# One tile place of eight in an input ring is loaded by two DMAs, of 120 and of 8 partitions

## The chip, the core and the metric

The kernel runs on one core of one Trainium2 chip. The metric is the device time of one execution in microseconds. Five engines with their own instruction streams work side by side: PE (TensorE, with its weight load PEld), DVE (VectorE), ACT (ScalarE), POOL (GpSimd) and SP (SyncE), which here only issues DMAs and waits. The core has 16 DMA engines that all queues share.

## The reference, cut to what matters

```python
def ref(inputs):                                   # inputs: (2048, 64, 256) float32
    Z = jnp.einsum('bnd,bmd->bnm', inputs, inputs) # a 64x64 Gram matrix per batch
    li, lj = jnp.tril_indices(n, k=-1)             # n = 64: strictly below the diagonal
    return Z[:, li, lj]                            # (2048, 2016)
```

## The kernel before, in words

The input is 134.2 MB (128 tiles of 1 MB), the output 16.5 MB. A tile is 16 batches: 128 partitions, each with 8 joined rows of 256 floats, which is one run of 8 KB in DRAM. `x_joined` is the input seen in this way, so that tile t is rows `t * PARTS` to `(t + 1) * PARTS`.

**Loads.** SP issues one DMA a tile (L151) into place `k = t % 8` of the ring `x_in`. The ring has eight places, each with a semaphore `loaded[k]` that the DMA raises by 16. From tile 8 on, SP waits before each load until DVE has turned the tile that used the place before (L147). Tiles 4 and 5 wait for the multiplications of tiles 0 and 1 (`LATE`, L150).

**DVE.** `turn(t)` waits for `loaded[k]` (L195), then for PE to be done with the tile that used this place of `x_turned` three tiles earlier (L197), and transposes the tile in 32x32 blocks from `x_in` to `x_turned` (L198). From tile 11 on, `turn_rows` follows every second tile: it transposes one of four pieces of a group's products (L215). A group is eight tiles.

**PE.** A hardware loop of 43 laps with three tiles each; the places of tiles run over 129, of which the first is blank. A tile is 256 matmuls (L252), placed side by side in the array. PE waits for `turned[j]`, and before the end of a set for the other PSUM set to be emptied.

**ACT** copies the products out of PSUM (`keep`, L279), packs part of the rows into `packed_rows` (`pack`, L120 and L126) and issues two store DMAs a group (L137). **POOL** carries the parts that change partitions (L131). The last group's stores are issued by SP in four DMAs.

The order of work on each engine is written out in the program. What changes lies in SP's `load` and in the wait of DVE's `turn`.

Of the kernel before, what the change touches and what calls it, by code (L numbers as in the profile page):

```python
# [7 lines left out]
PARTS = 128  # L8
# [6 lines left out]
def first_column(i):  # L15

    return i * (i - 1) // 2


def gram_lower_triangle(nc: bass.Bass, x: bass.AP, y: bass.AP):  # L20
# [10 lines left out]
    TILE = SIDES * PER_SIDE  # L31
    TILES = BATCHES // TILE
    IN_RING = 8


    LATE = {4: 0, 5: 1}
# [29 lines left out]
    x_joined = x.rearrange("b (i r) d -> (b i) (r d)", r=JOINED)  # L66

    with ExitStack() as stack:  # L68
        def sbuf(name, shape):
            return stack.enter_context(nc.sbuf_tensor(name, shape, F32))  # L70

        def semaphore(name):
            return stack.enter_context(nc.semaphore(name))

        x_in = sbuf("x_in", [PARTS, IN_RING, JOINED * DIM])

# [9 lines left out]

        loaded = [semaphore(f"loaded{k}") for k in range(IN_RING)]

# [13 lines left out]
        def place(t):  # L102

            return divmod(t + BLANK, LAP)

        def set_of(j):

            return (0, j) if j < SET_TILES[0] else (1, j - SET_TILES[0])

        def piece_rows(piece):  # L110
            return slice(ROWS - (piece + 1) * PIECE, ROWS - piece * PIECE)

        def wait_packed_free(engine, group):

            if group >= 2:
                engine.wait_ge(stored[group % 2], group // 2 * STORES)
# [11 lines left out]
        def carry_across(copy, group, i, side):  # L128

            first, at = side * HALF, first_column(i)  # L130
            return copy(packed_rows[first:first + BLOCK, group % 2, :, at + BLOCK:at + i],  # L131
                        row_halves[first + BLOCK:first + HALF, i, :, 0:i - BLOCK])

        def store(engine, group, columns):
            rows = y[group * GROUP:(group + 1) * GROUP, columns].rearrange("(h q s) c -> s q h c", h=RUNS, s=SIDES)
            for side in range(SIDES):
                engine.dma_start(rows[side],  # L137
                                 packed_rows[side * HALF:side * HALF + BLOCK, group % 2, :, columns]).then_inc(
                    stored[group % 2], 16)

        @block.sync
        def _(sync):
            def load(t):
                k = t % IN_RING
                if t >= IN_RING:
                    lap, j = place(t - IN_RING)
                    sync.wait_ge(turned[j], (lap + 1) * LAP)  # L147
                elif t in LATE:
                    lap, j = place(LATE[t])
                    sync.wait_ge(tile_multiplied[j], (lap + 1) * ARRAY_TILES)  # L150
                sync.dma_start(x_in[:, k], x_joined[t * PARTS:(t + 1) * PARTS]).then_inc(loaded[k], 16)  # L151

            for t in range(TILES):
                load(t)

            group, long_rows = GROUPS - 1, first_column(BLOCK)
            sync.wait_ge(packed_home, group * PIECES + LONG_PIECES)
            sync.wait_ge(packed_across, (group + 1) * LONG_PIECES)
            sync.wait_ge(last_carried, 1)
            store(sync, group, slice(long_rows, PACKED))  # L160
            sync.wait_ge(packed_home, GROUPS * PIECES - 1)
            sync.wait_ge(last_packed, 1)
            store(sync, group, slice(0, long_rows))
            for b in range(2):
                groups = (GROUPS - b + 1) // 2
                sync.wait_ge(stored[b], (groups + (1 if group % 2 == b else 0)) * STORES)
# [23 lines left out]
        @block.vector  # L190
        def _(dve):
            def turn(t):

                k, (lap, j) = t % IN_RING, place(t)
                dve.wait_ge(loaded[k], (t // IN_RING + 1) * 16)  # L195
                if lap > 0:
                    dve.wait_ge(tile_multiplied[j], lap * ARRAY_TILES)  # L197
                nc.vector.transpose(  # L198
                    x_turned[:, j].rearrange("p c b s (h u n v) -> p u v (c b s h) n", h=ROWS // BLOCK, u=PAIRS, v=PAIR),
                    x_in[:, k]).then_inc(turned[j], LAP)  # L200

            def turn_rows(n):
                group, piece = divmod(n, PIECES)
                rows = piece_rows(piece)
                if piece == 0:

                    lap, j = place((group + 1) * GROUP_TILES - 1)
                    s = set_of(j)[0]
                    dve.wait_ge(kept[s], (lap + 1 + s) * LAP)
                if group > 0:  # L210

                    dve.wait_ge(packed_home, n - PIECES + 1)
                    if piece < LONG_PIECES:
                        dve.wait_ge(packed_across, (group - 1) * LONG_PIECES + piece + 1)  # L214
                nc.vector.transpose(  # L215
                    row_halves[:, rows].rearrange("p i h (n u v) -> p (i h) u n v", u=PAIRS, v=PAIR),
                    products[:, group % KEPT_RING, rows, :].rearrange("p i (h q) -> p (i h) q", q=BLOCK)).then_inc(
                    rows_turned, 1)

            for j in range(BLANK):  # L220
                nc.vector.memset(x_turned[:, j, 0:CHUNKS // 2], 0.0).then_inc(turned[j], 1)  # L221
            turned_rows = 0
            for t in range(TILES):
                turn(t)
                if t >= PIECE_LAG and (t - PIECE_LAG) % 2 == 0:
                    turn_rows(turned_rows)
                    turned_rows += 1
            for n in range(turned_rows, GROUPS * PIECES):
                turn_rows(n)
            wait_packed_free(dve, GROUPS - 1)  # L230
            dve.wait_ge(rows_turned, (GROUPS - 1) * PIECES + LONG_PIECES)
            for i in range(BLOCK + 1, ROWS):
                last = carry_across(nc.vector.tensor_copy, GROUPS - 1, i, 1)
            last.then_inc(last_carried, 1)
# [105 lines left out]
```

## Time and profile before

| What | Value |
|---|---|
| Median of 3 runs | 417.86 us (416.99 to 419.29) |
| Profiled execution, its own time | 417.85 us |
| Its span, first to last instruction | 416.1 us |
| Mean granted TensorE clock | 0.959 |
| Busy: PE, PEld, DVE | 377.6, 370.4, 364.5 us |
| Busy: ACT, POOL | 178.8, 199.9 us |
| Moved by DMA | 151.01 MB, mean 363 GB/s |

The span is what the trace covers; 1.75 us of the execution's own time lie around it. Times in rows are microseconds from the span's start. Releasers (after `<-`) are what ended an engine's idle time. Busy shares are averages over a start, a long middle and an end that have different limits, so the stretches have to be read one by one.

### The profile page before, as it was taken

To read this page: it belongs to the slowest core of one execution; us is meant where nothing else is said; L and a number is where in the kernel's file an instruction comes from. 1 tells how busy PE (TensorE), PEld (TensorE's weight loads), DVE (VectorE), ACT (ScalarE), POOL (GpSimd) and SP (SyncE) were. 2 spreads that over 40 slices of the span, in tenths; PEclk is the share of its full clock that TensorE was granted. 3 is DMA by queue.
4 is the path that set the end of the run, shared out by engine and by line. 5 is a ranking of instruction groups with operands and counts; after the bars stand their busy time and mean duration, and the time that the engine had idled before them with its cause. 6 is when DMAs were issued, how large, how long until landed. Compare 5 with 4: busy or idle time off the path is not lost.

```text
span 416.1 us, 68691 instructions
## 1 busy us (share of the span) xinstructions
PE 377.6 (91%) x33024; PEld 370.4 (89%) x33024; DVE 364.5 (88%) x224; ACT 178.8 (43%) x829; POOL 199.9 (48%) x981
## 2 busy tenths in 40 slices
PE   4469999999999999999999999999999899899940
PEld 4469999999999999999999999999999899898940
DVE  3438899999999999999999998999979799797964
ACT  0011134434555434554345543455544445444465
POOL 1000084664818283564828183563808356182783
PEclk9559999999999999999999999999999999999985
DMA  8259999999999999999999999999999999995218
GB/s 325 87 181 425 426 419 425 418 423 421 420 421 423 423 421 421 422 420 423 380 423 399 388 419 411 403 380 415 347 425 338 422 382 358 392 326 247 68 50 199
DMA packets 21178, 151.01 MB, mean 363 GB/s; under 512 B 2592, under 2 KB 2720, under 8 KB 4768
## 3 DMA queue, kind: packets, MB, share of 16 engines
q1 hardware_dynamic: 18752, 135.26, 81.3%
q10 hardware_dynamic: 2400, 15.48, 9.9%
q14 instruction: 20, 0.16, 0.1%
q8 instruction: 6, 0.10, 0.1%
HBM read 134.22 MB, written 16.52 MB: 362 GB/s over the span
## 4 chain that ended last, share of the span: by engine, by line
PE 55%; DMA 31%; DVE 5%; issue 5%; ACT 2%; ACTq 0%; DVEq 0%
PE bank_set L252 55%; DMA x_in<-x_dram 31%; DVE x_turned L198 4%; ACT packed_rows L120 1%; DVE row_halves L215 1%; ACT packed_rows L126 1%; DVE x_turned L221 0%; ACTq L137 0%; ACT products L279 0%; DVEq L197 0%; ACTq L68 0%; DVEq L214 0%; ACTq L294 0%; ACTq L270 0%
## 5 line engine op out<-in xcount | busy, mean ns | idle before, releaser
L252 PE MATMUL bank_set<-x_turned 32*64 32x64 f32 x33024 | 377.6, 236 | 22.7 <-issue 11.9
L252 PEld LDWEIGHTS bank_set<-x_turned 32*64 32x64 f32 x33024 | 370.4, 132 | 29.8 <-issue 22.6
L198 DVE STREAM_TRANSPOSE x_turned<-x_in 128x2048 f32<-128x2048 f32 x128 | 292.0, 2290 | 41.2 <-PE bank_set L252 18.0
L131 POOL COPY packed_rows<-row_halves 32x60 f32<-32x60 f32 (+30 forms) x961 | 196.4, 206 | 209.2 <-DVE row_halves L215 171.6
L279 ACT COPY products<-bank_set 128x512 f32<-128x512 f32 (+1 forms) x91 | 68.6, 760 | 208.6 <-PE bank_set L252 189.3
L215 DVE STREAM_TRANSPOSE row_halves<-products 128x1024 f32<-128x1024 f32 x64 | 77.1, 1207 | 3.2 <-ACT products L279 2.7
L120 ACT COPY packed_rows<-row_halves 128x32 f32<-128x32 f32 (+30 forms) x481 | 62.8, 220 | 0.0
L126 ACT COPY packed_rows<-row_halves 128x128 f32<-128x128 f32 x256 | 56.9, 300 | 4.3 <-issue 3.0
L279 ACT ACT_TABLE_LOAD x1 | 1.3, 1283 | 19.9 <-PE bank_set L252 19.9
L131 DVE COPY packed_rows<-row_halves 32x2 f32<-32x2 f32 (+30 forms) x31 | 3.4, 187 | 0.0
L120 POOL COPY packed_rows<-row_halves 128x2 f32<-128x2 f32 (+14 forms) x15 | 2.3, 210 | 0.1
L221 DVE MEMSET x_turned<- 128x1024 f32 x1 | 0.9, 912 | 1.0 <-PEq L334 1.0
L172 POOL MEMSET x_turned<- 128x1024 f32 x1 | 1.0, 952 | 0.4 <-POOLq L334 0.4
L334 POOL MEMSET const-float32-0.0<- 128x1 f32 x1 | 0.1, 99 | 0.2 <-issue 0.2
L334 POOL MEMSET const-bfloat16-1.0<- 128x1 bf16 x1 | 0.1, 102 | 0.0
L334 POOL MEMSET const-uint8-127<- 128x1 uint8 x1 | 0.1, 102 | 0.0
L334 POOL MEMSET const-float32-1.0<- 128x1 f32 x1 | 0.1, 99 | 0.0
## 6 DMA issues: line engine op xcount, KB each, us to landing
x_in<-x_dram SPq DMA_DIRECT2D x128, 1024.0 KB, 17.3
y_dram<-packed_rows ACTq DMA_DIRECT2D x30, 504.0 KB, 8.1
y_dram<-packed_rows SPq DMA_DIRECT2D x2, 380.0 KB, 3.9
y_dram<-packed_rows SPq DMA_DIRECT2D x2, 124.0 KB, 3.6
```

Of the source, the lines that this page charges most:

```text
L120: return copy(packed_rows[:, group % 2, :, at:at + i], row_halves[:, i, :, 0:i])
L126: return copy(two[:, :, :, 0:BLOCK], row_halves[:, i:i + 2].rearrange("p w h j -> p h w j"))
L131: return copy(packed_rows[first:first + BLOCK, group % 2, :, at + BLOCK:at + i], row_halves[first + BLOCK:first + HALF, i, :, 0:i - BLOCK])
L172: nc.gpsimd.memset(x_turned[:, j, CHUNKS // 2:CHUNKS], 0.0).then_inc(turned[j], LAP - 1)
L198: nc.vector.transpose(x_turned[:, j].rearrange("p c b s (h u n v) -> p u v (c b s h) n", h=ROWS // BLOCK, u=PAIRS, v=PAIR), x_in[:, k]).th ...
L215: nc.vector.transpose(row_halves[:, rows].rearrange("p i h (n u v) -> p (i h) u n v", u=PAIRS, v=PAIR), products[:, group % KEPT_RING, row ...
L221: nc.vector.memset(x_turned[:, j, 0:CHUNKS // 2], 0.0).then_inc(turned[j], 1)
L252: done = nc.tensor.matmul(bank_sets[s][side * HALF:(side + 1) * HALF, g, at, :].rearrange("r (n u v) -> r u n v", u=PAIRS, v=PAIR), rows, ...
L279: last = nc.scalar.copy(products[:, group % KEPT_RING, :, in_group * PER_SIDE:(in_group + count) * PER_SIDE].rearrange("p i (m g b) -> p i ...
L334: nc = bacc.Bacc("TRN2", target_bir_lowering=False, num_devices=1)
```

## The change

The tile in place 4 of the ring (tiles 4, 12, ..., 124: 16 of the 128) is loaded by two DMAs from SP, one right after the other: partitions 0 to 119, then 120 to 127. Both raise the same semaphore by 16, and DVE's wait counts 32 a lap for this place. Everything else stays.

```diff
+    SPLIT, AHEAD = 4, 120
...
-                sync.dma_start(x_in[:, k], x_joined[t * PARTS:(t + 1) * PARTS]).then_inc(loaded[k], 16)
+                first = t * PARTS
+                if k == SPLIT:
+                    sync.dma_start(x_in[0:AHEAD, k], x_joined[first:first + AHEAD]).then_inc(loaded[k], 16)
+                    sync.dma_start(x_in[AHEAD:PARTS, k], x_joined[first + AHEAD:first + PARTS]).then_inc(loaded[k], 16)
+                else:
+                    sync.dma_start(x_in[:, k], x_joined[first:first + PARTS]).then_inc(loaded[k], 16)
...
-                dve.wait_ge(loaded[k], (t // IN_RING + 1) * 16)
+                dve.wait_ge(loaded[k], (t // IN_RING + 1) * (32 if k == SPLIT else 16))
```

## Rows read from the trace of the kernel before

**Rows 1.** The page, part 2: the span in 40 slices, busy tenths and GB/s

```profile
PE   4469999999999999999999999999999899899940
DVE  3438899999999999999999998999979799797964
DMA  8259999999999999999999999999999999995218
GB/s 325 87 181 425 426 419 425 418 423 421 420 421 423 423 421 421 422 420 423 380 423 399 388 419 411 403 380 415 347 425 338 422 382 358 392 326 247 68 50 199
```

**Rows 2.** The chain that ended last, in order of time: start, length, what

```profile
36.81 8.63 PE bank_set L252 x422
45.44 0.12 issue
...
229.56 5.99 PE bank_set L252 x294
...
241.32 20.79 DMA x_in<-x_dram
...
366.00 21.77 DMA x_in<-x_dram
...
391.67 8.83 PE bank_set L252 x423
```

**Rows 3.** The tile x_in, its instructions and landings, stretch 280:400

```profile
L198 DVE STREAM_TRANSPOSE x_turned<-x_in x38: 2268/2272/2315, 280.0 to 394.0; 128x2048 f32<-128x2048 f32 x38
  DMA x_in<-x_dram: 6.9, 7
DMA to landing us min/median/max: 19.7/21.6/24.7
```

**Rows 4.** The tile x_in, its landings, stretch 75:100

```profile
DMA to landing us min/median/max: 12.5/13.5/15.5
```

**Rows 5.** Windows: columns named in the first line; share of the 16 DMA engines

```profile
core 0: us, PE busy (x) PEld busy (x) DVE busy (x) ACT busy (x) POOL busy (x), PEclk, DMA share, GB/s
180.00:200.00 20.00, 19.76 (x1775) 19.50 (x1773) 19.38 (x11) 8.36 (x41) 10.21 (x49) 1.00 1.01 422
24.30:26.50 2.20, 0.47 (x29) 0.28 (x19) 0.00 (x0) 0.00 (x0) 0.00 (x0) 0.50 0.05 22
383.00:384.00 1.00, 1.00 (x121) 1.00 (x107) 1.00 (x1) 0.00 (x0) 0.00 (x0) 1.00 0.06 25
391.00:392.00 1.00, 0.88 (x85) 0.75 (x72) 1.00 (x2) 0.39 (x3) 0.84 (x5) 1.00 0.06 25
```

**Rows 6.** DMA packets in the stretch 383:391

```profile
DMA packets 29, 0.21 MB, mean 27 GB/s; under 512 B 3, under 2 KB 3, under 8 KB 3
```

**Rows 7.** The page, parts 2 and 3: packets and queues of the whole span

```profile
DMA packets 21178, 151.01 MB, mean 363 GB/s; under 512 B 2592, under 2 KB 2720, under 8 KB 4768
q1 hardware_dynamic: 18752, 135.26, 81.3%
q10 hardware_dynamic: 2400, 15.48, 9.9%
q14 instruction: 20, 0.16, 0.1%
```

**Rows 8.** SP's own waits and its issue of loads over the span

```profile
SPq L151 <- DVE x_turned L198: 301.1, 116, 4.7
L151 SPq DMA_DIRECT2D x_in<-x_dram x128: 327/328/662, 0.7 to 371.5; - x128
```

**Rows 9.** All engines in order of time, stretch 0:45; idle before in brackets

```profile
26.53 18.72 PE L252 MATMUL bank_set<-x_turned 32*64 32x64 f32 x1551 [1.75 <-issue]
...
27.65 2.31 DVE L198 STREAM_TRANSPOSE x_turned<-x_in 128x2048 f32<-128x2048 f32 x1 [5.42 <-PE bank_set L252]
```

**Rows 10.** DVE in order of time, stretch 396:416.1

```profile
401.20 3.75 DVE L215 STREAM_TRANSPOSE row_halves<-products 128x1024 f32<-128x1024 f32 x3 [2.69 <-ACT products L279]
```

## The prediction

> **What bounds the kernel now.** I read the slices of the page first [rows 1]. After a start of some 30 us, PE and the DMA engines are both at 9 tenths, and DVE nearly so, up to about 380 us. But in the last third PE and DVE have slices at 8 and 7 tenths, while GB/s falls from a flat 420 to values between 338 and 425. Three resources that are all "busy" need the chain to tell them apart.
>
> The chain [rows 2] has two parts. From 36.81 to 229.56 us it is PE alone: 22 laps of three tiles, (229.56 - 36.81) / 22 = 8.761 us a lap, 2.920 us a tile, with 0.12 us of loop issue in each. PE is the bound there, at a granted clock of 1.00 [rows 5]. From 241 us on the chain is loads: pieces of 21 to 22 us from the issue of a load to its landing. Lap 42, the last, starts at 391.67. From 229.56 that is 162.11 us for 18 laps (two laps lie before 36.81, then 22, 18 and the last make 43), or 9.006 us a lap instead of 8.761. So the second part lost 162.11 - 18 x 8.761 = 4.41 us to late loads. That the loads are late and not DVE is seen in the turns: 38 turns start between 280.0 and 394.0 us, 114.0 / 37 = 3.08 us apart, while DVE idled 6.9 us for loads [rows 3].
>
> **Why loads are late although the DMA engines still move data quickly.** A load took 13.5 us from issue to landing between 75 and 100 us [rows 4] and 21.6 us after 280 [rows 3]. SP issues as soon as a place is free, so this is the age of a load in a ring of eight tiles. Such a growth can't come from a mean rate: at 422 GB/s [rows 5] a tile of 1.049 MB takes 2.485 us, under PE's 2.920. With a group's stores (2 x 64 x 8,064 B = 1.032 MB, 2.45 us) eight tiles need 8 x 2.485 + 2.45 = 22.3 us against PE's 23.4. The mean has 1 us to spare in a group; one member has not. The end of the load stream shows it. The last load is issued at 371.5 [rows 8]. From 383 to 392 the share of the 16 DMA engines is 0.06, at 25 GB/s [rows 5]: 1/16 = 0.0625, one DMA engine alone. In 383:391 it moves 26 packets of 8 KB and 3 completion packets [rows 6], 8 / 26 = 0.308 us each: full speed for one, since 422 / 16 = 26.4 GB/s is 0.310 us for 8 KB. So the other 15 are done with all tiles while one still has about 10 us of work, some four tiles. The same signature stands at 24.30:26.50, share 0.05 [rows 5], in the early tile that is issued alone. I call it the late engine. A tile counts as landed only with its share, so the late engine sets DVE's time.
>
> Its pace: 8 x 3.08 = 24.6 us for eight tiles, of which 64 load packets take 64 x 0.308 = 19.7; the other 4.9 are 8 store packets and what it loses besides. That is 1.3 us over PE's 23.4. It falls behind in every group, the ring hides it until about 235 us, and then it leads.
>
> **What the change does.** Packets are one partition row each: 128 loads x (128 rows + 16 completions) and 4 stores x (64 + 16) give 18752, the count of q1 [rows 7]. So a whole tile is 8 rows on each of 16 engines. The trace has no load of 120 rows. Bounds for what the late engine carries of a split tile: nothing (120 = 15 x 8, the grain of the whole tile kept, and one engine left out), or 9 rows (the same, and one of the 8 single rows on top). In the first case it saves 8 x 0.308 = 2.46 us in eight tiles, in the second it gets 0.31 more. I keep both ends and choose the first; the second and the middle are rivals.
>
> The Trainium skill, "DMA: Bandwidth & Descriptors", section "Why a DMA increments its semaphore by 16 and not by 1", says that a DMA is spread over the largest number up to 16 that divides the slowest dimension, on the lowest-numbered engines. By it, 120 rows go to engines 0 to 14 and the 8 rows to engines 0 to 7, one each; engine 15 gets none. No row here carries an engine's number. The same page, in "Latency and other measured facts", calls engines 7 and 15 usually slower: if the late one is 15 the sum is the first end, if it is 7 the second.
>
> *The late engine, first end:* 24.6 - 2.46 = 22.1 us for eight tiles, under PE's 23.4 by 1.3 us; the loss per group is gone, and the lag never fills the ring.
>
> *The engines with 9 rows:* mean pace 22.3 + 0.31 = 22.7 us. The page puts q10 at 9.9% of 416.1 us, 41.2 us for 30 stores [rows 7], 1.37 us each instead of 1.22, so 2.75 in a group: 8 x 2.485 + 0.31 + 2.75 = 22.9 us. It is under 23.4, by 0.4 us.
>
> *SP:* one more issue of 0.33 us in eight tiles, 16 in all [rows 8]. SP is waiting 301.1 us for DVE [rows 8]; behind the second issue stands the next load, whose place comes free 2.9 us later, and loads are issued 12 us and more before DVE wants them. Cost nothing; if that cover were gone, 0.33 us for each of 16 tiles, 5 us. The further completion packets are a few ns each.
>
> *DVE:* the wait only counts to 32, no instruction more. It waits for the later of two landings. The 8 rows are queued right behind the 120, so they are a packet's time late, 0.3 us, hidden by the ring's age of 13 us. The Trainium skill, same page, "Rules for kernel authors", speaks against such a pair: it wants 128 partitions and 1 MiB in a DMA and says that two transfers to disjoint partitions bring nothing. By it only the 0.3 us a split tile and no gain would be left, the rival "no change".
>
> *Start:* tiles 0 to 3 are not split. DVE turns tile 4 at 27.65, released by PE and not by the load, and PE works without a break from 26.53 on [rows 9], so an earlier landing of tile 4 is worth nothing. *End:* after PE's last lap (391.67 + 8.83 = 400.50) come ACT's copy, four turns of rows on DVE from 401.20 [rows 10], packing and stores, 416.1 - 400.5 = 15.6 us, none of it a load. It moves as a block.
>
> *DVE as next bound:* for eight tiles 8 x 2.272 [rows 3] and four turns of rows of 1.25 (3.75 us for three, [rows 10]) are 23.2 us, close to 23.4. But in 180:200, where no load is late, DVE does just this with 19.38 of 20 us busy [rows 5] and PE keeps its pace. So PE leads to the end.
>
> **Sum.** PE's last lap starts at 229.56 + 18 x 8.761 = 387.26 instead of 391.67. The span becomes 416.1 - 4.4 = 411.7, and the execution's own time 417.85 - 4.4 = 413.4 us. The profiled execution's time is the median's (417.86), so no further shift.
>
> **The rivals.**
> - *The late engine is among those with 9 rows (slower).* It is at work without a break from about tile 5 until 392.5, so each packet more moves the end of its work: 15 x 0.31 = 4.7 us. PE's last laps hang on it, 422.5 us. For: nothing in the rows says which engine is late, and eight of 16 would carry more. It decides as soon as the late engine's share of a split tile is above 8. Against: it would have to be one of those eight.
> - *Its share stays at 8, or the split is spread otherwise and relieves nobody in particular:* 417.9 us. For: seven of the 16 are in this place in the likeliest split.
> - *The late engine is relieved, but those with 9 rows take over.* Needs 0.5 us in a group beyond my 22.9: for example the 20 instruction packets [rows 7] falling on them, or the unexplained loss at stores. Each 0.15 us over 23.4 costs about 2 us over 15 groups: 415.5 us.
> - *Too little relief:* it needs 1.3 of the 2.46 us, five rows of eight, to be under PE. With four rows taken off, 24.6 - 1.23 = 23.4, the gain is still nearly whole.
>
> **How the numbers follow.** Late engine left out and PE leads: 0.70, 413.4, own range 412.3 to 414.8. Relieved but with a new leader: 0.05, 415.5. No change: 0.11, 417.9. Slower: 0.14, 422.5. The 0.70 is a judgement: no row gives an engine's number, and a blind draw would make it 1 in 16. I put it far higher because both facts single out one engine: one alone of 16 is late all through the run, and the likeliest split leaves out one alone, at an end of the row. A measurement of this kernel can tell about 0.5%, 2.1 us. Faster 0.74 (the first two), same 0.12, slower 0.14. The range runs from 412.3 to 418.5 and leaves out the slower case and little else. The low end adds 1 us for the tail, where POOL's carries could start earlier.
>
> **What would show it.** Completion packets: 2592 under 512 B now, 162 DMAs x 16; with 15 + 8 instead of 16 in each of 16 tiles it should be 2592 + 16 x 7 = 2704; with 16 in each, 2848. The chain should be laps of 8.76 us up to the last, starting near 387.3. The turns after 280 should be 2.92 us apart, waits for loads near nothing, and the age of loads after 280 no longer above that of 75:100. The stretch with share 0.06 before the last landing should be gone. If share 0.06 lasts longer than 10 us, the slower rival is right; if 24.6 us for eight tiles stays, the second. A short share of 8/16 at the end would be the engines with the ninth row.

## The result and the profile after

The changed kernel takes 490.6 us (median of 6 runs, 486.0 to 493.0), the kernel before 417.5 us beside it: ratio 1.174, 95% interval 1.170 to 1.178. It is 73 us slower; forecast were 413.4 us and a range up to 418.5. The profiled execution took 486.0 us, its span is 484.2. Where a result below says "one run", a second run was left out because the chip was in a slower state.

The page of the kernel after, part 2, same columns as [rows 1], with the granted clock:

```profile
PE   4579998989979797888887797879978787897960
DVE  4348697969687787968587794878779687886974
PEclk8569999997999899889989898998989999898995
DMA  8369999999999999999999999999999999999136
GB/s 338 86 224 420 296 403 291 420 316 413 285 403 319 382 294 384 321 343 363 299 372 250 377 290 319 378 247 400 267 388 327 315 366 256 391 276 349 53 87 171
```

The row to read is GB/s. The DMA engines are as busy as before, 9 tenths throughout, but from the fifth slice to the sixteenth the rate alternates between about 290 and 400, one slice each. A slice is 12.1 us, two are 24 us, about eight tiles: once in a lap of the ring the same engines take longer for the same bytes. A busy share doesn't show this; busy share and GB/s side by side do.

The chain of the kernel after, in order of time (start, length, what):

```profile
57.37 2.32 DVE x_turned L206
60.10 21.05 DMA x_in<-x_dram
81.15 1.42 issue
82.56 2.32 DVE x_turned L206
...
397.05 1.14 issue
398.19 2.32 DVE x_turned L206
...
459.70 8.84 PE bank_set L260 x426
```

Loads lead from 32.8 us on (75% of the span), not from 241 [rows 2]. The step from one turn of a split tile to the next is (398.19 - 57.37) / 12 = 28.4 us for eight tiles, against PE's 23.4 and the late engine's 24.6. PE's last lap starts at 459.70 instead of 391.67 [rows 2]: 68.0 us later, the whole difference of the spans (484.2 - 416.1 = 68.1). The tail moved as a block, as forecast.

Windows around the second split tile, tile 12, in the kernel after (columns as in [rows 5]):

```profile
45.00:48.00 3.00, 2.83 (x266) 2.70 (x257) 2.70 (x2) 1.13 (x2) 0.00 (x0) 1.00 1.01 415
48.00:51.00 3.00, 3.00 (x292) 3.00 (x280) 1.74 (x1) 0.00 (x0) 0.00 (x0) 1.00 1.07 208
51.00:54.00 3.00, 3.00 (x292) 3.00 (x285) 1.71 (x1) 0.66 (x1) 0.00 (x0) 1.00 1.04 197
54.00:57.00 3.00, 2.86 (x272) 2.73 (x261) 1.73 (x2) 0.94 (x2) 1.02 (x5) 1.00 0.94 339
```

For six microseconds all 16 engines are busy at half the rate, 208 and 197 GB/s. The packets and the waits of the kernel after:

```profile
DMA packets 21290, 151.01 MB, mean 312 GB/s; under 512 B 2704, under 2 KB 2832, under 8 KB 4880
q1 hardware_dynamic: 18864, 135.26, 82.8%
PEld bank_set L260 <- DVE x_turned L206: 65.6, 52, 2.6
DVE x_turned L206 <- issue: 59.0, 38, 3.5
```

The bytes are the same and the completion packets are 2704, the number forecast for 15 + 8 engines in each split tile. So the spread over the engines was as the first end of my bounds assumed; what it costs was not. DVE's 59.0 us "issue" are waits for loads that the profile gives no releaser for: each of the 38 ends 0.08 us after a landing in the place that DVE turns next. Only 14 of them, 17.2 us, stand before split tiles; 24, 41.8 us, stand before whole ones. The whole tiles are late as well. PE now waits for DVE, and after it starved a lower clock is granted, as in this stretch of the kernel after:

```profile
438.00:440.00 2.00, 0.11 (x8) 0.11 (x16) 2.00 (x2) 1.31 (x5) 1.68 (x9) 0.90 1.01 396
440.00:442.00 2.00, 2.00 (x142) 2.00 (x145) 2.00 (x2) 0.00 (x0) 1.01 (x6) 0.50 1.00 407
```

PE works 0.11 of 2 us, and the next 2 us are granted at 0.50, the lower of the clock's two levels (1.2 of 2.4 GHz). Its busy time grew from 377.6 to 392.6 us.

### The profile page after: what moved, and what is told of

Same layout as the page of the kernel before. It is cut to its first block, busy times and chain, and to the rows that moved or that the text cites. A ratio compares the mean times of both kernels' runs of the same rounds, so it can differ in the third digit from the quotient of the medians.

```text
span 484.2 us, 68707 instructions
## 1 busy us (share of the span) xinstructions
PE 392.6 (81%) x33024; PEld 381.2 (79%) x33024; DVE 366.0 (76%) x224; ACT 179.3 (37%) x829; POOL 198.2 (41%) x981
## 2 busy tenths in 40 slices
DMA packets 21290, 151.01 MB, mean 312 GB/s; under 512 B 2704, under 2 KB 2832, under 8 KB 4880
## 4 chain that ended last, share of the span: by engine, by line
DMA 75%; DVE 8%; issue 7%; PE 6%; ACT 2%; SPq 1%; ACTq 0%; DVEq 0%
DMA x_in<-x_dram 75%; DVE x_turned L206 7%; PE bank_set L260 6%; ACT packed_rows L123 1%; SPq L156 1%; ACT packed_rows L129 1%; DVE row_halves L223 1%; SPq L159 0%; DVE x_turned L229 0%; ACTq L140 0%; ACT products L287 0%; ACTq L71 0%; DVEq L205 0%; ACTq L302 0%; ACTq L278 0%
## 5 line engine op out<-in xcount | busy, mean ns | idle before, releaser
L260 PE MATMUL bank_set<-x_turned 32*64 32x64 f32 x33024 | 392.6, 242 | 75.8 <-DVE x_turned L206 58.3
L260 PEld LDWEIGHTS bank_set<-x_turned 32*64 32x64 f32 x33024 | 381.2, 137 | 87.0 <-DVE x_turned L206 65.6
```

The costliest lines, as they stand in the source:

```text
L260: done = nc.tensor.matmul(bank_sets[s][side * HALF:(side + 1) * HALF, g, at, :].rearrange("r (n u v) -> r u n v", u=PAIRS, v=PAIR), rows, ...
```

## The experiments

All kernels are the kernel before with one edit in SP's `load` (and the count in DVE's wait). Ratios are to the kernel before on the same chip; the chips differ between groups of runs. `PIECES_OF` lists the pieces that place 4 is loaded in, `aside` is a tensor that nobody reads. The diffs are cut to the line that matters. The expectations speak of ports: SBUF, the on-chip memory that holds `x_in`, is reached through ports that each serve certain partitions, and the theory is that DMA engines which write one port at the same moment share its rate. The mapping follows in the point on the step that failed.

**1. Which of the two DMAs costs: 120 alone, 128 + 8, 112 + 16, 64 + 64.**

```diff
                 if k == SPLIT:
+                    for a, b in PIECES_OF:    # e1: (0,120); e2: (0,128); e3: (0,112),(112,128); e4: (0,64),(64,128)
+                        sync.dma_start(x_in[a:b, k], x_joined[first + a:first + b]).then_inc(loaded[k], 16)
+                    # e2 only: 8 rows more
+                    sync.dma_start(aside[120:128], x_joined[first:first + 8]).then_inc(loaded[k], 16)
...
```

> Place 4 is loaded by the 120-partition DMA alone; partitions 120 to 127 of that place are loaded once, with tile 4, and left out afterwards (15 of 16 tiles). Theory A: the DMA of 120 partitions is itself slow, because its packets take about twice their time (in the changed kernel's trace half the stretches run at 200 GB/s, the others at 420). Then most of the loss stays: 465 to 490 us. Theory B: the DMA of 8 partitions is what hurts. Then this one goes back to 413 to 419 us. Theory C: two DMAs on one semaphore, or the wait for 32, cost the time: back to 413 to 419 us as well.

e1: 479.1 us (one run; the kernel before 417.2). 120 alone keeps some 62 of the 73 us.

> Place 4 is loaded whole by one DMA of 128, and a second DMA brings 8 rows more to a tensor that nobody reads; DVE waits for both. Theory A (the 120 is slow): 417 to 424 us, the 8 rows cost a packet or so on the engines that carry them. Theory B (the 8 are slow): 450 us and more. Theory C (two DMAs on one semaphore): 450 us and more.

e2: 426.3 us, ratio 1.021 (1.015 to 1.028). 2 us above theory A's range. The 8 rows cost 9.1 us, not 4.7, but a small part of the loss; two DMAs on one semaphore are no cause of the rest. 62 + 9 = 71, nearly the 73.

> Place 4 is loaded by DMAs of 112 and of 16 partitions; both divide by 16, so completion packets should be 32 a split tile (2848 under 512 B in all). Theory A1: a DMA is slow when its rows don't spread over all 16 engines (120 on 15). Then 112 and 16 are both fine: 415 to 421 us. Theory A2: a DMA is slow when its share of rows for each engine is a contiguous block that doesn't match how the partitions are joined to the memory's ports; only the whole tile of 128 is laid out to match. The Trainium skill, 'SBUF — State Buffer', section 'Door 1', gives the mapping; by it 112 in blocks of 7 collides often. Then this kernel is slow as well: 440 to 490 us.

e3: 471.7 us (one run), completion packets 2848: 16 engines for both DMAs, and slow all the same. Theory A1 (too few engines) falls.

> Place 4 is loaded by two DMAs of 64 partitions, 0 to 63 and 64 to 127, each on 16 engines with 4 rows. Theory A1 (fewer than 16 engines is what is slow): 415 to 421 us, no loss. Theory A2 (ports): by the skill's mapping partitions 0 to 63 reach only half of the ports, and so do 64 to 127, so each DMA runs at half speed: the tile takes about 5 us instead of 2.5 and the kernel 450 to 480 us. Completion packets 2848 in both.

e4: 484.5 us, ratio 1.161 (1.147 to 1.174), completion packets 2848. The windows from 48 to 54 us in this run:

```profile
48.00:51.00 3.00, 3.00 (x288) 3.00 (x283) 2.28 (x1) 0.20 (x1) 0.00 (x0) 1.00 1.09 243
51.00:54.00 3.00, 3.00 (x292) 3.00 (x281) 1.26 (x1) 0.48 (x1) 0.00 (x0) 1.00 0.98 218
```

Half the rate again, with all 16 engines carrying 4 rows each. What is left is where the rows go, or where they are read from.

**2. Same source rows, same count, another destination.** The kernel before, with extra rows beside each tile of place 4.

```diff
+                if k == SPLIT:      # (a, b): e5 (32,96), e6 (32,92), e7 (0,60), e8 (0,64)
+                    sync.dma_start(aside[a:b], x_joined[first:first + b - a]).then_inc(loaded[k], 16)
```

> The kernel before, with 64 rows more beside each tile of place 4, loaded from the tile's first 64 rows to partitions 32 to 95 of a tensor nobody reads. 16 engines get 4 rows each. Ports theory (blocks of 4 partitions, 32 to 95 reach all 16 ports, one for each engine): packets stay at 0.31 us, the late engine has 4 more in eight tiles, 1.23 us, so 15.4 x 1.23 = 19 us more: about 436 us, and GB/s stays at 420 in the first half. Rival (any DMA that is not 128 partitions is slow): stretches at 200 to 300 GB/s and 450 us or more.

e5: 437.3 us, ratio 1.050 (1.046 to 1.053), 1 us over the value forecast from 0.31 us a packet. The second of these windows in this run:

```profile
51.00:54.00 3.00, 3.00 (x292) 3.00 (x281) 3.00 (x3) 1.01 (x1) 0.61 (x3) 1.00 1.00 415
```

> The same 64 source rows, to partitions 0 to 63, 16 engines with 4 rows each. Ports theory: 16 engines on 8 ports, packets at 0.62 us, 2.5 us in eight tiles on every engine, the late one too: 15.4 x 2.5 = 38 us more than before, 450 to 460 us. If only the number of engines counts, or the source: 436 us as with 32 to 95.

e8: 480.5 us, ratio 1.151 (1.148 to 1.155). The same window:

```profile
51.00:54.00 3.00, 3.00 (x293) 3.00 (x283) 2.30 (x2) 0.00 (x0) 0.00 (x0) 1.00 1.06 268
```

The two kernels differ in nothing but the partitions that the extra rows go to, 32 to 95 or 0 to 63: 20 us against 63 us over the kernel before. So the slow packets come from the SBUF side of the transfer, neither from the DRAM reads nor from a count. The size was missed (450 to 460 forecast).

> As the run with 32 to 95, but 60 rows to partitions 32 to 91: 15 engines with 4 rows, one with none. Two things are told apart. If the late engine is the one left out, its pace doesn't change and the others go from 22.6 to about 24 us in eight tiles: 418 to 424 us. If it is one of the 15: 436 us, as with 64 rows. If a DMA on 15 engines is slow by itself, GB/s falls below 350 in stretches and the time is 450 us or more.

e6: 436.4 us, ratio 1.048 (1.044 to 1.051), the same as with 16 engines. Fifteen engines are not slow in themselves. And the one that got nothing isn't the late one: had it been, the forecast was 418 to 424 us.

> The same 60 source rows, to partitions 0 to 59. Ports theory: 15 engines write 8 ports, so the packets take about 0.6 us, 2.4 us in eight tiles for 15 engines instead of 1.2: slower than the run to 32 to 91 by 15 to 20 us, with stretches at 200 GB/s. If the side of the DRAM reads is what counts, the same time as to 32 to 91, since the source is the same.

e7: 448.7 us (one run), 12 us over the same rows to 32 to 91. The sign is as forecast, the size (15 to 20) is not. Nor does any run explain why 60 rows to 0 to 59 cost 32 us and 64 rows to 0 to 63 cost 63: one engine and four rows less, and half the loss.

**3. A split tile with half of its rows placed well.**

> Place 4 is loaded by three DMAs: partitions 32 to 95, 0 to 31, 96 to 127, each on 16 engines. Ports theory: the first reaches all 16 ports at full speed, each of the others 8 ports. The run with 64 rows more to 0 to 63 cost 63 us, the one with 64 rows more to 32 to 95 cost 20 us: the collisions of 64 rows are worth 43 us, and here 64 rows collide and none are added: 417 + 43 = 460 us, between the kernel before and the 484.5 us of 64 + 64. If every DMA that isn't the whole tile is slow: 484 us or more. If what counts is the number of engines: 417 us.

e13: 448.8 us, ratio 1.076 (1.073 to 1.080). Between 417 and 484 as the ports theory has it, but 11 us under its number: here 64 colliding rows cost 31.5 us, in 64 + 64 they cost 67.3 / 2 = 33.6 us, in the extra rows 43 us.

**4. Which engine is late.** Four DMAs of m rows with a partition step of 4, so that by the ports theory no two engines meet; completion packets show m engines in each (2592 + 64 m, as 3104 for m = 8).

```diff
+                if k == SPLIT:
+                    for j in range(4):
+                        sync.dma_start(aside[32 + j:32 + 4 * m:4], x_joined[t * PARTS:t * PARTS + m]).then_inc(loaded[k], 16)
...
```

> The kernel before, and with each tile of place 4 four extra DMAs of 8 rows to partitions 32 + j, 36 + j, ... of a tensor nobody reads (8 ports, so no two engines on one). By the Trainium skill, 'DMA: Bandwidth & Descriptors', 'Why a DMA increments its semaphore by 16 and not by 1', 8 rows run on the first 8 engines, so each of those gets 4 packets more, the others none. If the late engine is one of the first 8: 15.4 x 1.23 = 19 us more, 436 us, as with 64 rows. If it is in the other half: near 418 to 424 us.

> The same with 7 rows in each of the four DMAs: the first 7 engines get 4 packets more. If the run with 8 rows is at 436 us and the late engine is the eighth (number 7, which the Trainium skill, 'DMA: Bandwidth & Descriptors', 'Latency and other measured facts', calls usually slower, as 15): this one falls back to 417 to 424 us. If the late engine is among the first seven, it stays at 436 us.

8 rows (e9) 436.6 us, ratio 1.042 to 1.049; 7 rows (e10) 436.7 us, 1.044 to 1.050. The eighth engine isn't the late one either.

> As the runs with four extra DMAs of 8 and of 7 rows (436.6 and 436.7 us), with 2 rows in each: by the Trainium skill's rule ('DMA: Bandwidth & Descriptors', how many engines) they run on the first two engines. If the late engine is one of those two: 436 us. If not: 417 to 422 us.

> The same with 4 rows in each, on the first four engines. If the late engine is one of the first four: 436 us, else 417 to 424 us.

> The same with 6 rows in each, on the first six engines. If the late engine is one of the first six: 436 us. If it is the seventh: 417 to 424 us. If all four runs of this kind are at 436 us whatever the number, it isn't the engine that carries the packets, but the extra DMAs themselves (four more in one place, on one semaphore).

> Four extra DMAs of 5 rows with each tile of place 4. With 2 and 4 rows the time was 425 us, with 6, 7 and 8 rows 437 us. If the late engine is the fifth: 436 to 437 us; if it is the sixth: 425 us. In the second case the loads don't lead the chain late in the run.

2 rows (e14) 425.2 us, ratio 1.018 to 1.021; 4 rows (e15) 424.6 us, 1.015 to 1.020; 5 rows (e17) 440.0 us, 1.051 to 1.060; 6 rows (e16) 437.1 us, 1.046 to 1.051. The step lies between 4 and 5. The runs with 2 and 4 rows came out above their forecast (up to 422 and 424 us), the one with 5 rows 3 us above it. The landings after 280 us show it as well, first with 4 rows, then with 5:

```profile
DMA to landing us min/median/max: 13.1/15.4/17.0
```

```profile
DMA to landing us min/median/max: 19.9/23.4/29.0
```

With 4 rows loads hardly age (13.5 us was the age at 75:100 in the kernel before, [rows 4]), with 5 they do: the late engine is the fifth of the 16, if the engines are taken in the order that the Trainium skill's rule gives (lowest numbers first). Two limits remain. The runs with 4 and 6 rows were on one chip, the run with 5 on another, so "fifth" rests on its being the same engine on both. And the fifth row always goes to partitions 48 to 51, so what is late may be the engine or the place that it writes; no run separates them.

With 2 and 4 rows the time is PE's, yet 7 to 8 us over the kernel before. In the chain with 2 rows about one lap of three is longer:

```profile
54.10 9.32 PE bank_set L257 x428
63.42 0.12 issue
63.54 8.65 PE bank_set L257 x427
72.19 0.12 issue
72.31 9.48 PE bank_set L257 x435
```

After 45 us the chain has 14 such laps, and each of them holds one of the 14 stretches of 2.4 us in which SP issues the four extra DMAs (54.62, 78.54, 102.82 us and so on); no other lap holds one. The run with 4 rows shows the same, while the single extra DMA of e2 leaves the laps at 8.64 us. 14 laps of 0.7 us are 10 us, less the 4.4 us that late loads no longer cost: that is the difference of the spans, 421.8 to 416.1. How issuing them slows PE isn't shown; its granted clock is 1.00 in the five of these laps that I read.

**5. Is the lag what the kernel before loses at its end.** Only the ring's length is changed.

```diff
-    IN_RING = 8
+    IN_RING = 10      # and 9 in the other run
```

> The kernel before with a ring of 9 places instead of 8, no split. If the loss of 4.4 us in the last third is a lag of one engine that the ring can hide for so long, one place more hides one tile time more, 2.9 us: 414.5 to 416 us. If the loads are late for lack of bandwidth, a place more changes nothing: 417 to 418 us.

e11: 415.2 us (10 runs), ratio 0.995 (0.993 to 0.997), as forecast.

> The kernel before with a ring of 10 places, no split. Lag theory: 5.8 us more can be hidden, more than the 4.4 us that are lost, so PE leads to the end: 413 to 414.5 us, with the chain in laps of 8.76 us up to the last. Bandwidth theory: no change, 417 to 418 us.

e12: 414.1 us, ratio 0.993 (0.990 to 0.995), as forecast. This is the fastest kernel of the study, 3.3 us under the kernel before and 1.1 under the ring of 9. The chain of the run with 10 places:

```profile
309.16 8.66 PE bank_set L252 x424
317.82 0.12 issue
317.94 6.00 PE bank_set L252 x298
...
326.40 29.24 DMA x_in<-x_dram
...
388.34 8.86 PE bank_set L252 x427
```

PE leads until 324 us instead of 235 [rows 2], and its last lap starts 3.3 us earlier. Loads still lead at the end, so "up to the last" was too much. The late engine is still alone there:

```profile
381.00:382.00 1.00, 1.00 (x114) 1.00 (x109) 1.00 (x2) 0.00 (x0) 0.00 (x0) 1.00 0.06 25
```

**6. One split tile.**

```diff
+                if t == 60:        # the change's two DMAs, for this tile alone
...
```

> The changed kernel's split for one tile only (tile 60 of 128), the others whole. The split of 16 tiles cost 73 us, 4.6 us each. If each costs the late engine the same, which is at work without a break, one split moves the end of its work by 3.5 to 4.6 us: 421 to 422 us. If the loss is something that only builds up over many splits, or that PE's granted clock adds when PE starves: 417 to 419 us.

e18: 423.5 us, ratio 1.016 (1.012 to 1.020): one split costs 5.7 us, more than the 4.6 us that a sixteenth of 73 is, and over the forecast of 421 to 422. Its chain:

```profile
167.67 3.14 PE bank_set L259 x165
...
178.97 23.12 DMA x_in<-x_dram
```

It shows that two things are paid. From the turn of tile 52 to that of the split tile 60 are 26.6 us for eight tiles instead of the 23.4 of the kernel before: 3.2 us for the split itself. And the split uses up what the ring still hid: loads lead from 171 us on instead of 235, and the next eight tiles each time take 24.2 to 25.3 us. The other 2.5 us go with the late engine leading earlier. So a single split costs at once, without many before it, but its 5.7 us isn't the price of every split.

## Why the prediction was wrong, point by point

- **What bounds the kernel before: right.** PE to 235 us, then one late engine. Its pace of 24.6 us is a mean: from 287 us on the turns in place 4 are 24.8 to 25.1 us apart, eight tiles each. The ring of 10 gives back 3.3 of the 4.41 us that I took from the chain, and at 0.06 share that engine is seen alone in it too.
- **How a split tile spreads: right.** 2704 completion packets are 15 + 8. The Trainium skill's rule ("DMA: Bandwidth & Descriptors", "Why a DMA increments its semaphore by 16 and not by 1") agrees with the completion packets here and in every run with another count: 16 + 16 for 112 + 16, 15 for 60, and 8, 7, 6, 5, 4 and 2 for as many rows.
- **"In the first case it saves 8 x 0.308", and "The engines with 9 rows: mean pace 22.3 + 0.31": this is the step that failed.** I priced every row of the 120 at the 0.308 us of a row in a whole tile. The windows show about 200 instead of 422 GB/s with all engines busy, so about 0.65 us; in the trace the median packet of 8 KB from 48 to 54 us took 0.62 us, in the kernel before 0.31. A row's price depends on which partitions the engines write at the same moment. The Trainium skill, "SBUF — State Buffer", "Door 1: The DMA port swizzle", says that partitions share 16 ports, four neighbours and the four 32 further on one port, and 64 further the other of a pair; "DMA: Bandwidth & Descriptors", "The descriptor swizzle", says that a load of 128 is dealt out so that each engine has a port to itself. The runs agree with it: with 64 rows to 32 to 95 (all 16 ports by the Trainium skill's mapping) the window has 415 GB/s, to 0 to 63 (8 ports) 268, from the same source. Blocks of 8 neighbours for each of 15 engines meet in pairs by that mapping, if the engines go through their rows in step. That the engines take neighbouring partitions in a load that is not 128 is inferred from these rates; no row names an engine's partition. I had read these pages and weighed only the rule on the number of engines.
- **The late engine left out (0.70): wrong as well.** The run with 60 rows, which leaves out the same engine, costs as much as with 64. It is the fifth as far as the runs tell, and the change gives it a ninth row. So even without collisions the sum would have been that of the slower rival, 422.5 us, not 413.4, and e2 measured 426.3 for nine rows. By my own count one engine of 16 was relieved and eight got more; 0.70 against 0.14 had no measurement under it. The Trainium skill's "usually slower" engines 7 and 15 are not the late one here; the same row ("DMA: Bandwidth & Descriptors", "Latency and other measured facts") ties this as a best guess to DMAs whose descriptors software writes, and these loads are on a hardware queue ("hardware_dynamic" in [rows 7]). I had left that half of the row out. (The first two chances, 0.70 and 0.05, also add up to 0.75 and not 0.74.)
- **The slower rival: right in its sign and its ground, not in its size.** It asked for nine rows on the late engine and named 4.7 us; e2, which gives it just that, cost 9.1, and the change 73.
- **"The 8 rows are ... a packet's time late, 0.3 us": too small.** The extra 8 rows of e2 cost 9.1 us, 0.6 us in eight tiles. Their eight engines write partitions 120 to 127, two ports by the Trainium skill's mapping. In e2's trace 26 packets of 8 KB that start between 48.6 and 50.0 us took 0.5 to 1.27 us instead of 0.31, though only 8 of them can be extra rows: rows of the whole tiles beside them are slowed too.
- **Size of the loss.** From tile 12's turn (52.19 us before, 57.37 after) to the last lap are 113 tiles, 14.1 times eight: 24.1 us each before, (459.70 - 57.37) / 14.1 = 28.5 us after. 4.4 x 14.1 = 62, with the 5.2 before tile 12 it is the 68 us. Of this, half rate alone explains 8 x 0.31 = 2.5 us in eight tiles and the 8 rows 0.6. The other 1.3 lie in the packets too. From tile 28 to tile 116 each engine spends on average 25.8 us in 8 KB packets for eight tiles, in the kernel before 21.4: 4.4 us more, of 4.9 that eight tiles take longer there. And 239 packets in eight tiles took over 0.45 us, 34 in the kernel before, where the split tile has 128 rows. So some 80 rows of whole tiles are slowed as well. PE's lower clock isn't needed for this. Why whole tiles are hit, engines out of step or another reason, isn't shown, nor why the price differs between runs (33.6, 31.5 and 43 us for 64 rows, where 4 packets x 0.31 x 15.4 = 19 were due).
- **DVE's count, start and tail: right**, they cost nothing that shows. **SP: "Cost nothing" is not shown.** SP's issue of the 120 rows now stands in the chain 14 times, 0.35 us each but for the first with 0.47 (1.0% of the span, 5 us), where the chain of the kernel before has none of it. The DMA engines are at 9 tenths all the while, so it need not have cost anything; no run separates it.

## What to carry to other kernels

Price a DMA by its partitions, not by its bytes alone: a tile of 128 partitions ran at 422 GB/s, windows of 3 us with pieces of 120, 112 and 64 from partition 0 at about 200 to 290, and with 64 from partition 32 at 415. Before moving work off a late DMA engine, find out which it is; extra rows on the first m engines, for several m, tell. If one engine lags steadily and the rest has room, a longer ring hides it: two more places were worth 3.3 us here, while the split cost 73.

## What was not expected of the hardware

One of 16 DMA engines, the fifth as far as the runs tell, falls over 1 us behind PE's pace in eight tiles; the seven runs that bear on its position fit this, though only those with 4, 5 and 6 rows fix it. 64 more rows beside each tile of place 4 cost 20 or 63 us over the run, by their first partition alone. A slow small DMA also slows the packets of whole tiles beside it. A split of a single tile costs 5.7 us. And four small extra DMAs on the first 2 or 4 engines lengthen just those laps of PE in which SP issues them, from 8.65 to 9.4 us, without any wait for loads; the cause stays open.
